# Where VectorE forms its half of group 3 in a chunk of a fused dynamic-convolution and selective-scan kernel

## The reference

```
pooled = x.mean(axis=(2, 3))                # -> attention weights, one depthwise 3x3 kernel per image
y  = depthwise3x3(x * ch_att, agg_w)
y1 = y @ b1_w.T + b1_b ;  y2 = y @ b2_w.T + b2_b
g  = gelu(y1) * y2 ;  x = x + layernorm_over_channels(g)

xh, z = split(x @ W_in) ;  xh = silu(causal_conv_k2(xh))
dt_low, Bmat, Cmat = split(xh @ W_x) ;  dt = softplus(dt_low @ W_dt + b_dt)
h = exp(dt * A) * h + dt * Bmat * xh        # scan over the 4096 pixels, 256 channels x 16 states
out = ((h . Cmat) + xh * D) * silu(z) @ W_out
x = silu(group_norm(out)) + x
```

## Time and profile before

| | |
|---|---|
| Median of 3 runs (lowest to highest) | 14103.46 us (14099.97 to 14105.63) |
| The profiled execution's own time | 14102.87 us |
| Its span in the trace | 14101.0 us |
| DVE, POOL, ACT, PE busy | 96%, 94%, 86%, 79% |
| Mean granted clock of TensorE | 0.872 of full speed |
| Mean length of a chunk (span / 256) | 55.1 us |

### The profile page before, as it was taken

The page is one execution under the profiler, slowest core; times in us unless marked ns, Lnnn a source line. Parts: engine busy times, 40 slices in busy tenths (PEclk is TensorE's granted clock), DMA queues, the critical chain, the costliest instruction groups (busy, mean ns, idle before and its releaser), DMA issues.

```text
span 14101.0 us, 163967 instructions
## 1 busy us (share of the span) xinstructions
PE 11209.7 (79%) x33024; PEld 3328.2 (24%) x33024; DVE 13476.1 (96%) x12083; ACT 12099.3 (86%) x24489; POOL 13248.2 (94%) x3076
## 2 busy tenths in 40 slices
PE   7788777787787878778787878777787878788787
PEld 2222222222222222222222222222222222222221
DVE  7999999999999999999999999999999999999999
ACT  7888888888888888888888888888888888888888
POOL 6999999999999999999999999999999999999999
PEclk8888888888888888888888888888888888888887
DMA  5656565556656565655566565655556565656555
GB/s 131 144 137 143 140 150 137 144 138 145 144 142 145 136 147 141 145 139 142 141 146 145 138 147 136 149 138 143 143 139 145 143 144 137 145 138 148 140 140 118
DMA packets 1068261, 1992.06 MB, mean 141 GB/s; under 512 B 123649, under 2 KB 124730, under 8 KB 1067066
## 3 DMA queue, kind: packets, MB, share of 16 engines
q1 hardware_dynamic: 1065786, 1979.41, 58.7%
q10 hardware_dynamic: 1280, 0.02, 0.0%
HBM read 1626.62 MB, written 352.32 MB: 140 GB/s over the span
## 4 chain that ended last, share of the span: by engine, by line
POOL 56%; issue 35%; DVE 4%; ACT 3%; PE 2%; POOLq 0%; ACTq 0%; DVEq 0%; DMA 0%; SPq 0%
POOL hq L973 40%; POOL dbx L965 16%; DVE hq L861 2%; ACT ps_a L592 1%; DVE dbx L844 1%; PE ps_acc L417 0%; PE ps_b L405 0%; PE pp L384 0%; ACT dbx L606 0%; ACT L552 0%; PE pp L325 0%; PE pp L361 0%; DVE pp L820 0%; POOLq L963 0%; PE pp L376 0%
## 5 line engine op out<-in xcount | busy, mean ns | idle before, releaser
L973 POOL TENSOR_TENSOR hq<-hq,c_rep 128x2048 f32<-128x2048 f32 x2048 | 9258.7, 4537 | 740.9 <-ACT carry L611 733.2
L861 DVE TENSOR_TENSOR_SCAN hq<-ps_a,dbx 128x512 f32<-128x512 f32 x8192 | 9442.4, 1204 | 122.4 <-ACT dbx L606 79.8
L592 ACT ACTIVATE ps_a<-dt_rep,A_neg 128x512 f32<-128x512 f32 x8192 | 5627.3, 687 | 1463.7 <-DVE hq L861 1408.5
L965 POOL TENSOR_TENSOR dbx<-dtx_rep,b_rep 128x2048 f32<-128x2048 f32 (+1 forms) x1024 | 4080.8, 3985 | 90.9 <-DMA dtx_rep<-dtx_d 90.9
L844 DVE TENSOR_TENSOR dbx<-dtx_rep,ps_b 128x2048 f32<-128x2048 f32 (+1 forms) x1280 | 2626.6, 2052 | 244.9 <-PE ps_b L405 244.9
L606 ACT ACTIVATE dbx<-ps_a,dbx,carry 128x1 f32<-128x1 f32 x7168 | 2504.0, 349 | 238.6 <-POOL dbx L965 137.1
L417 PE MATMUL ps_acc<-hq,dsum 128*32 128x512 f32 x16384 | 2356.5, 649 | 167.7 <-POOL hq L973 165.6
L325 PE MATMUL pp<-xin,diag 128*128 128x504 f32 (+3 forms) x4608 | 2214.0, 608 | 6.0 <-ACT diag L637 6.0
L405 PE MATMUL ps_b<-dbl,bsel 41*128 41x512 f32 x2560 | 1476.2, 657 | 373.6 <-DVE dbx L844 201.8
L361 PE MATMUL pp<-x,W_taps 128*128 128x512 f32 x768 | 660.6, 957 | 988.3 <-DVE x L815 639.2
L325 PEld LDWEIGHTS pp<-xin,diag 128*128 128x128 f32 x4608 | 793.2, 189 | 1398.4 <-issue 1398.4
(11 more groups left out here) (117 smaller groups left out, 9996.7 us busy)
## 6 DMA issues: line engine op xcount, KB each, us to landing
dtx_rep<-dtx_d SPq DMA_DIRECT2D x2048, 256.0 KB, 5.5
dt_rep<-dt_d SPq DMA_DIRECT2D x2048, 256.0 KB, 5.6
c_rep<-bc_d SPq DMA_DIRECT2D x1024, 256.0 KB, 5.5
b_rep<-bc_d SPq DMA_DIRECT2D x1024, 128.0 KB, 2.9
dtx_d<-sp SPq DMA_DIRECT2D x256, 512.0 KB, 2.8
dt_d<-dt SPq DMA_DIRECT2D x256, 512.0 KB, 6.0
out<-o SPq DMA_DIRECT2D x128, 512.0 KB, 3.5
xin<-in_x SPq DMA_DIRECT2D x192, 320.0 KB, 8.5
```

The lines of the kernel that those rows point to most:

```text
L592: A(ps_a[:, BANK[i], :], dt_rep[:, q // NQ, g, :], ACT.Exp, scale=A_neg[:, q // NQ, q % NQ, g:g + 1]).then_inc(exp_done, 1)
L861: v.tensor_tensor_scan(hq[:, q % HQ, g, :], ps_a[:, BANK[i], :], dbx[:, slot(q), g, :], 0.0, ALU.mult, ALU.add).then_inc(scan_done, 1)
L965: g.tensor_tensor(dbx[:, slot(q), m:, :], dtx_rep[:, d, m:, :], b_rep[:, c % 2, q % NQ // 2, :].unsqueeze(1).to_broadcast([P, DG - m, T]), ...
L973: g.tensor_tensor(quad, quad, c_rep[:, c % 2, q % NQ, :].unsqueeze(1).to_broadcast([P, DG, T]), ALU.mult).then_inc(cmul_done, 1)
```

## The change

`DVE_SHARED` goes from 7 to 8, and the call stands further down in the body for one tile: behind the gating of the chunk before. On VectorE the product of the two tiles of group 3, which stood between scan 7 and scan 8, now stands behind scan 8 and the output gating, before scan 9. No instruction is added or removed, nothing moves on the other four engines, and TensorE's select of group 3 stays at tile 6.

```diff
-PE_SHARED, DVE_SHARED = 6, 7
+PE_SHARED, DVE_SHARED = 6, 8
...
                 for u in range(NT):
                     s, g = divmod(u, DG)
                     scan(b, c, u)
-                    if u == DVE_SHARED:
-                        weigh_inputs(b, c, SHARED)
                     if g == 1 and s % 2:
...
                     if c and u == DVE_Y1:
                         y_gate(b, c - 1, 1)
+                    if u == DVE_SHARED:
+                        weigh_inputs(b, c, SHARED)
                     if u == DVE_Y0:
                         y_gate(b, c, 0)
```

## The result

The changed kernel takes **14144.12 us** (median of 9 runs, 14140.12 to 14145.5); the kernel before took 14102.77 (9 runs, 14098.85 to 14109.27). The ratio is 1.0028, 95% interval 1.0018 to 1.0039: slower by 0.28%. The forecast was 14134, and 14144 lies inside its range of 14096 to 14168. The span of the profiled execution grew from 14101.0 to 14138.6.

The account below looks back on a forecast made before the run. It took a ring through GpSimd, ScalarE, TensorE and VectorE as the bound. 3 x 0.17 + 3 x 0.23 - 0.19 - 0.04 = 0.97 us, times 32 = 31 us, gave 14134; range 14096 to 14168.

Parts of the forecast that it names:

- The hole moves in front of the gating: VectorE's wait leaves the product of group 3; the gating instead waits for TensorE's sum of group 7, starting 0.15 us after.
- Scan 9 starts 0.12 earlier: On VectorE in chunk 2, scan 9 behind the moved product starts at 7218.62 instead of 7218.74, 0.12 us earlier.
- Select 4 starts 0.23 later: TensorE's select of group 4 overwrites the bank the product reads, so starts at 7218.75 instead of 7218.52.
- ScalarE, VectorE and GpSimd hand it on: The 0.23 us delay passes through the projection to dt, ScalarE's and VectorE's softplus, and group 4's state copy to GpSimd.
- 0.06 to spare in chunks 1 to 3: GpSimd's start on group 4 has 0.06 us of room, so these chunks each lose 0.17 us of the 0.23.
- Chunk 4 gets 0.19 shorter, chunk 8 0.04: Chunk 4 sheds its product's 0.35 us lateness, limited by the first ring; chunk 8 has 0.27 us before VectorE's softplus.
- Chunks 5, 6, 7: 0.23: Taken like chunk 7, where GpSimd already idles for group 4's state copy, these chunks each pay the whole 0.23 us.
- a gating 0.49 behind its sum: Alternative delay from TensorE's sum to VectorE's gating, taken from chunk 4's product; 118 us more, giving 14221.
- The clock rival: TensorE's 0.28 us idleness before select 4 lowers its granted clock; 0.57 us a chunk, 14250; chance 0.02.
- The rival in which nothing is given back: All eight chunks pay the full 0.23 us, chunk 4's 0.35 staying; 59 us more, 14162; chance 0.14.
- The rival of the hole: VectorE's idle time before the product was the bound, so faster: 14061, or 13858 if closed in full; chance 0.09.
- the other ring: First ring: select 4, projection to dt, softplus, group 4's state copy, GpSimd; in chunk 2 0.06 us from the second.

Follow-up runs that it names:

- the reordered TensorE: Changed kernel with TensorE's select of group 4 moved behind the convolution taps of tiles 8 and 9; 14139.44 us, ratio 1.0028.
- both rings shortened: Against the kernel before: product behind scan 8 but ahead of the gating, and two convolution taps moved behind the projection to dt; 13923.0 us, ratio 0.9874.
- either edit alone: Kernel before with only the product behind scan 8, ahead of the gating: 14085.4 us; or only two taps behind the projection to dt: 14086.04 us.

## Why the prediction was right

Its steps, in their order, with what was measured:

- *The hole moves in front of the gating.* It did: 204.7 us there and 4.1 at the product. The gating starts 0.16 behind the sum, where 0.15 was taken from the product's own 0.14; the 0.06 of the last gating of the run, which would have given 14111, was not the right row.
- *Scan 9 starts 0.12 earlier.* It was 0.10, since the product comes 0.61 behind the gating's start, not 0.58, and the gating 0.01 later.
- *Select 4 starts 0.23 later.* It was 0.26, as the 0.01 of the gating and the 0.03 of the product add up (their ends rounded).
- *ScalarE, VectorE and GpSimd hand it on.* The waits of ScalarE (0.29 to 0.65), VectorE (a visible 0.33) and GpSimd (0.25) in chunk 2 show each step. The experiments show it from both sides: with the same hold of 0.26 and 1.7 us taken out of TensorE's run behind it, the loss is gone.
- *0.06 to spare in chunks 1 to 3.* Chunks 2 and 3 grew by 0.23 and 0.21, which with a hold of 0.26 leaves 0.04 to spare on average.
- *Chunk 4 gets 0.19 shorter, chunk 8 0.04.* -0.14 and +0.02, off by 0.05 and 0.06, of which 0.03 is the larger hold.
- *Chunks 5, 6, 7: 0.23.* +0.27, +0.14, +0.25. Chunk 6 lies below and chunk 1 above what was said. These are the two long chunks (56.46 and 65.17 us), and the prediction took them to be like chunks 7 and 2 without reading rows of either. Together they moved by 0.45 where 0.40 was said; how it is split between them was not followed up, and that the two misses nearly cancel is luck.

So the mechanism was right, and the sum came out 0.31 us an image too small (41 us instead of 31). About 8 x 0.03 of it is the longer hold and 3 x 0.02 the smaller room. These are the two terms that were mis-sized, the start of the product behind the gating above all.

Two readings of the prediction do not hold beside this. It said that a gating 0.49 behind its sum goes into the range, but the 14221 that it worked out for that lies above the range's end of 14168. And it gave TensorE 0.28 us of idleness before select 4 where its own hold was 0.23; the trace has 0.19. The clock rival, priced by that idleness, did not show: the granted clock is 1.00 from 7231 to 7245 in the changed kernel, and its mean over the run is 0.873, beside 0.872 before. The rival in which nothing is given back was wrong in chunk 4, whose 0.35 went away as said, though its 14162 is no farther from the result than 18 us. The rival of the hole, at 14061 or in full 13858, falls with the product ahead of the gating: no hole, and 16 us. The Trainium skill (Perfetto Trace Analysis, Optimization Strategy) says to find the gaps on the engine being optimized and to make what they wait for start sooner or finish faster. It puts no price on a gap. By that rule one comes to the kernel with select 3 one scan earlier, and this case bears it out in part: 67 us came of it, where the gap was 244.9. With the product ahead of the gating the gap was real too, 208 us of waiting less, but what follows VectorE had no use for the time. Only when the other ring had been shortened did the same edit give 163 us (14086.04 to 13923.0).

Left open: what held the gain of the earlier select 3 back in chunks 1, 3 and 8 of an image; what tells the chunks that fell to the low clock from the others; why the product of chunk 4 started 0.35 late before (the cause was not tried, only that it vanishes when other instructions stand in front of it); and what makes the matmuls of the reordered TensorE run 0.20 longer.

## What to carry to other kernels

Two rings that share an engine and differ by a few hundredths of a microsecond make an edit that shortens only one of them look worthless, and one that lengthens the longer of them harmful. Find both before judging an edit, and try the edit with the other ring shortened as well. Of an edit that moves an instruction on the busiest engine, ask first which buffer it frees and who stands in a queue behind that buffer's next writer: here 0.26 us on a bank's hand-over outweighed 0.10 us won on the engine itself. And the gap of the busiest engine is worth what its successor can use, which is read by comparing starts to the releaser's end at each hand-over, not from the sum of the waits.

## What the runs showed of the hardware

- The same matmuls take different time in different order: two taps to a select 1.90 us against 1.81 to the D product, and the D product 1.06 behind a select against 0.95 behind taps. The distance from select 3 to the projection to dt was 0.19 to 0.20 us longer for it in all 240 chunks counted, nearly as much as the 0.26 of the change itself.
- A wait of 1.55 us on TensorE was followed by the low clock in only 39 of 210 chunks, one of 1.30 us in none of 30, and one of 0.19 us in none of 240.
- With both rings shortened the low clock came up at a place where no other kernel here has it: 36 of 240 chunks ran some 1.6 us longer between select 3 and select 4, behind idle stretches of 2.09 and 1.15 us in the one looked at. With either edit alone none did.
- A VectorE instruction started 0.35 us late in one of the eight chunks of an image, in every image, with no releaser in the trace. With the gating and scan 8 ahead of it, it was on time.
